# Attention over windows, products with V: one matmul for both heads of a pair, half of the result left unused, and two engines that copy the halves out

## The chip, the cores and the metric

One core of a Trainium2 chip runs the whole program. The metric is the time of one execution on the device, in microseconds (us); lower is better. TensorE (PE) multiplies, VectorE (DVE) and ScalarE (ACT) do elementwise work and copy results out of PSUM, GpSimd (POOL) does elementwise work in SBUF, and DMA queues move data.

## The reference, cut to what matters

A block with plain attention comes first, then six layers of local attention and a feed-forward network (FFN) over 4 x 1024 tokens of 128 features. The attention of a layer has 16 heads of 64 features and windows of 32 tokens, each of which looks at its own window and the one before it (64 keys):

```python
qkv = x @ Wqkv                                   # 128 -> 3 * 1024
# l2norm of q and k, rotary tables, then for each head and window of 32 queries:
sim = jnp.einsum('bhwie,bhwje->bhwij', bq, bk2) * QK_SCALE
sim = jnp.where(mask, -jnp.finfo(sim.dtype).max, sim)
attn = jax.nn.softmax(sim, -1)
out = jnp.einsum('bhwij,bhwje->bhwie', attn, bv2)
return out.reshape(b, h, n, d)                   # then @ Wo
```

The FFN is a layer norm, `x @ W1`, `a * gelu(gate)` and `@ W2`, each with a residual.

## The kernel before, in words

**Units and steps.** A unit is one tile of 128 tokens (four windows) with eight of the 16 heads (an `oct`), that is, four pairs of heads. There are 32 tiles x 2 octs x 6 layers = 384 units (`STEPS`). Everything is a software pipeline written out by hand: in each step, every engine does its part of several units, each at another stage, and semaphores (`need(engine, name, value)`) tie the engines together. There is no scheduler; each engine executes its list in the order in which it is written.

**TensorE in a step.** The loop at L893 to L907 issues, in this order: the first half of the FFN (`ffn_up`, L871 and L876) in one step of eight; the Q projection (L747, three matmuls of 512 columns); `ffn_down` (L886) in one step of eight; the scores (L767); the transpose of q (L779); the transpose of the probabilities (L800); the V projection and the K projection (L747); the transpose of k (L787); `attend(step-5)` (L824), the product with V; `output(step-6)` (L840), the product with Wo, in every second step; and the means of the FFN (L850, L857), each in one step of eight. There are 48 blocks of the FFN.

**attend.** For a pair `a` of heads, a window parity `w2`, a head `r` and a window half `wh`, one matmul holds V of one head as the stationary operand (64 keys by 64 features, rows `wh*64`) and streams the 32 queries of that head. The result goes to the partitions `r*64` of bank `6 + wh`. All operands are float32, for which the hardware executes each matmul of the source as two loads of the stationary operand and two matmuls; the 32 matmuls of the source are 64 loads and 64 matmuls in the trace. Each uses a quarter of the array, 64 rows by 64 columns, and four successive ones use the four quarters.

**attended.** ScalarE copies the 128 x 512 result of unit `n` to `aoT` (L471) one step later, and counts `aot_ready`. TensorE waits for that count ahead of the next `attend`, of `output`, and of `ffn_up`, whose results go into the banks 6 and 7 as well.

**VectorE in a step.** In order: the reciprocal of a sum (L1109), the K half of the rotation (L1085 to L1087), parts of the FFN in one step of eight each, the residual (L1095, in every second step, waits for `output`), the sum of the probabilities (L1103), `guarded` (L1070), `ffn_gated` (L1138, one step of eight), the row maximum (L1115, waits for the scores), the subtraction (L1123), the Q half of the rotation and two sums of squares (L1061).

Of the kernel before, what the change touches and what calls it, by code (L numbers as in the profile page):

```python
# [18 lines left out]
ACT = mybir.ActivationFunctionType  # L19
AX = mybir.AxisListType  # L20

P = 128
# [45 lines left out]
def is_unit(n):  # L68
    return 0 <= n < STEPS


def build(nc, x, w_attn, b_qk, b_v, Wqkv, Wo, W1, W2, cols, b1_cols, gains, c_t, wmod, rot_tab, out):
    ctx = ExitStack()
    with ctx:
# [3 lines left out]
        def sem(name):  # L78
# [94 lines left out]
            wqkv_in wo_in w1_in w2_in  # L173
            sqq_ready sqk_ready ssq_ready ssk_ready sg_ready ln_ready rn_ready rotq_ready rotk_ready add_ready qkr_ready trq_ready trk_ready seed_ready bits_set
            q_ready qk_ready sim_ready max_ready sub_ready p_ready pt_ready pts_ready vp_ready vs_ready pv_ready
            ri_ready aot_ready wo_ready x_mid_ready rot_made wo_moved pn_ready xs_ready w_hi w_lo sum_ready
            f_x f_m f_xc f_sq f_v f_ln f_rs f_xn f_xnT f_gate f_a f_gel f_u f_y f_out
            y_ready y_tr yo_ready y_sent""".split()
        s = {n: sem(n) for n in names}
# [7 lines left out]
        def need(eng, what, value):  # L187
            if value > 0:
                eng.wait_ge(s[what], value)
# [188 lines left out]
        def _(act):  # L378
# [86 lines left out]
            def attended(n):  # L465
                if not is_unit(n):
                    return
                tp, oc = n // UPT % 2, n % UPT
                need(act, "pv_ready", n + 1)
                need(act, "wo_ready", n // UPT - 1)  # L470
                act.activation(aoT[:, tp, oc * PAIRS:(oc + 1) * PAIRS, :].rearrange("p a (h n) -> p a h n", h=2),  # L471
                               psum[:, 6:8, 0:256].rearrange("p h (a n) -> p a h n", n=64), ACT.Copy).then_inc(s["aot_ready"], 1)

            def inverse_norm(n):
                if not is_unit(n):
# [167 lines left out]
        def _(pe):  # L643
# [167 lines left out]
            def attend(n, ffn_in_67):  # L811
                if not is_unit(n):
                    return
                tp, oc = n // UPT % 2, n % UPT
                pe.wait_ge(vsh_in[n % 4], (n // 4 + 1) * 32)
                need(pe, "pts_ready", n + 1)
                need(pe, "aot_ready", n)
                if ffn_in_67 is not None:
                    pe.wait_ge(s["f_u"], ffn_in_67 * CH + CH)
                for a in range(PAIRS):  # L820
                    for w2 in range(2):
                        for r in range(2):
                            for wh in range(2):
                                mm = pe.matmul(bank[6 + wh][r * 64:r * 64 + 64, a * 64 + w2 * WIN:a * 64 + w2 * WIN + WIN],  # L824
                                               vwin[w2][wh * 64:wh * 64 + 64, tp, oc, (2 * a + r) * DH:(2 * a + r + 1) * DH],
                                               probT[wh * 64:wh * 64 + 64, a, w2 * 64 + r * WIN:w2 * 64 + r * WIN + WIN],
                                               start=True, stop=True)
                mm.then_inc(s["pv_ready"], 1)

            def output(n):  # L830
                if not is_unit(n) or n % UPT == 0:
                    return
                tp, tile = n // UPT % 2, n // UPT
                need(pe, "aot_ready", n + 1)
                need(pe, "vs_ready", min(n + 4, STEPS))
                need(pe, "x_mid_ready", tile)
                if tile % TILES == 0:
                    pe.wait_ge(s["wo_moved"] if tile else s["wo_in"], tile // TILES if tile else 16)
                for k in range(HEADS // 2):
                    mm = pe.matmul(bank[5][:, 0:P], wo[:, k, :], aoT[:, tp, k, :],  # L840
                                   start=(k == 0), stop=(k == HEADS // 2 - 1))
                mm.then_inc(s["wo_ready"], 1)
# [16 lines left out]
            def ffn_up(b):  # L859
                if b is None:  # L860
                    return
                step = (b + 2) * UNROLL + 4
                layer = b // BLOCKS
                pe.wait_ge(s["w1_in"], layer * 16 + 16)
                pe.wait_ge(s["f_xnT"], b + 1)
                need(pe, "f_u", b * CH)
                need(pe, "pts_ready", min(step - 5, STEPS))
                need(pe, "aot_ready", min(step - 5, STEPS))
                for ch in range(CH):
                    w = CW[ch]  # L870
                    pe.matmul(bank[FFN_BANKS[ch]][0:w, :], w1[:, DFF + ch * P:DFF + ch * P + w], ff_n[:, :],  # L871
                              start=True, stop=True).then_inc(s["f_gate"], 1)
                for ch in range(CH):
                    w = CW[ch]
                    pe.wait_ge(s["f_gel"], b * CH + ch + 1)
                    pe.matmul(bank[FFN_BANKS[ch]][0:w, :], w1[:, ch * P:ch * P + w], ff_n[:, :],  # L876
                              start=True, stop=True).then_inc(s["f_a"], 1)
# [43 lines left out]
        def _(dve):  # L921
# [142 lines left out]
            def guarded(n):  # L1064
                if not is_unit(n):
                    return
                need(dve, "ssq_ready", n + 1)
                need(dve, "ssk_ready", n + 1)
                need(dve, "ln_ready", n)
                dve.tensor_reduce(ssg[:, :], ssq[:, :, :], AX.X, ALU.max).then_inc(s["sg_ready"], 1)  # L1070
# [18 lines left out]
            def residual(n):  # L1089
                if not is_unit(n) or n % UPT == 0:  # L1090
# [4 lines left out]
                dve.tensor_tensor(x_mid[:, col + 1:col + 1 + P], bank[5][:, 0:P], xs_in[:, col + HIST:col + HIST + P],  # L1095
                                  ALU.add).then_inc(s["x_mid_ready"], 1)

            def probability_sum(n):
                if not is_unit(n):
                    return  # L1100
                need(dve, "p_ready", n + 1)
                need(dve, "pn_ready", n - 1)
                dve.tensor_reduce(psumr[:, n % 2, 0, :], prob[:, n % 2, :, :], AX.X, ALU.add).then_inc(s["sum_ready"], 1)  # L1103
# [28 lines left out]
            def ffn_gated(b):  # L1132
                if b is None:
                    return
                for ch in range(CH):
                    w = CW[ch]
                    dve.wait_ge(s["f_a"], b * CH + ch + 1)
                    dve.scalar_tensor_tensor(out=gel[0:w, ch, :], in0=bank[FFN_BANKS[ch]][0:w, :],  # L1138
                                             scalar=b1_col[0:w, b // BLOCKS, 0, ch:ch + 1], in1=gel[0:w, ch, :],
                                             op0=ALU.add, op1=ALU.mult).then_inc(s["f_u"], 1)  # L1140
# [11 lines left out]
            for step in range(STEPS + 2 * UNROLL):  # L1152
                inverse_sum(step - 5)
                rotation(step - 1, 1)
                ffn_centred(block_at(step, 1))
                ffn_out(block_at(step, 5))
                residual(step - 7)
                probability_sum(step - 4)
                guarded(step - 1)
                ffn_gated(block_at(step, 4))  # L1160
                row_maximum(step - 3)
                below_maximum(step - 3)
                rotation(step, 0)
                square_sum(step, 0)
                square_sum(step, 1)
# [76 lines left out]
```

## Time and profile before

| | |
|---|---|
| median of three runs | 3431.78 us (3429.99 to 3432.28) |
| the profiled execution | 3432.49 us, span 3430.7 us |
| granted TensorE clock, mean | 0.987 |
| PE matmul / PE weight load busy | 96% / 75% of the span |
| DVE / ACT / POOL busy | 77% / 78% / 69% |
| matmuls and loads of the product with V (L824) | 24576 of each |

The span is the time from the first to the last instruction; the time of the run is 1.8 us more. "PE" are matmuls and "PEld" the loads of the stationary operand, which can go on beside a matmul. A busy PE isn't yet a PE at its peak, since the recorded time of a matmul includes the way through the array: a matmul that is recorded with 219 ns can be followed by another on the same quarter after much less than that. The rates must be read from starts, not from durations.

### The profile page before, as it was taken

What the parts mean: (1) busy time and instruction counts of PE and PEld (TensorE: products, weight loads), DVE (VectorE), ACT (ScalarE), POOL (GpSimd) and SP (SyncE); (2) the same over time, 40 slices, a digit from 0 to 9 for tenths busy, and PEclk for the clock granted to TensorE, in tenths of its full rate; (3) what the DMA queues carried; (4) which work ended last, traced back from release to release, by engine and by line L of the source; (5) the groups of instructions that cost most, each with busy time, mean ns of one, the idle gap of its engine ahead of it and who ended that gap; (6) DMA issues with size and microseconds to landing.
All of it is one profiled execution on the core that took longest, in us unless ns stands there. A gap on an engine that the chain in (4) does not pass through costs nothing. (4 is left out here: it accounts for less than half of the span.)

```text
span 3430.7 us, 124638 instructions
## 1 busy us (share of the span) xinstructions
PE 3290.3 (96%) x50165; PEld 2578.9 (75%) x50165; DVE 2628.7 (77%) x5823; ACT 2683.1 (78%) x5501; POOL 2361.1 (69%) x1568
## 2 busy tenths in 40 slices
PE   7979999999999999999999999999999999999997
PEld 5758777777777777777777777777777777777774
DVE  4558878878878877887877887877788777788783
ACT  3438888888888887888888888888888888888884
POOL 2028767777777776776777777777677677777771
PEclk9989999999999999999999999999999999999998
DMA  2001111211111211111211211121111121111111
GB/s 85 2 6 50 44 37 46 68 39 50 42 41 45 69 41 39 53 44 36 71 42 38 53 43 40 43 67 44 44 46 43 39 71 39 47 44 45 41 40 46
DMA packets 98187, 156.44 MB, mean 46 GB/s; under 512 B 18128, under 2 KB 39632, under 8 KB 96720
## 3 DMA queue, kind: packets, MB, share of 16 engines
q1 hardware_dynamic: 93440, 132.73, 14.3%
q10 hardware_dynamic: 4176, 15.74, 1.4%
q8 instruction: 402, 6.59, 0.8%
q14 instruction: 169, 1.38, 0.1%
HBM read 20.48 MB, written 2.10 MB: 7 GB/s over the span
## 5 line engine op out<-in xcount | busy, mean ns | idle before, releaser
L314 POOL TENSOR_TENSOR qks<-work 128x1024 f32<-128x1024 f32 x384 | 910.0, 2370 | 72.0 <-issue 62.8
L322 POOL TENSOR_TENSOR qkr<-qks,rnorm 128x1024 f32<-128x1024 f32 x384 | 731.4, 1905 | 321.0 <-issue 296.9
L330 POOL TENSOR_TENSOR probn<-prob,psumr 128x512 f32<-128x512 f32 x384 | 400.6, 1043 | 390.5 <-DVE psumr L1109 390.5
L498 ACT ACTIVATE sq<-psum 128x512 f32<-128x512 f32 x768 | 464.9, 605 | 184.1 <-PE psum L747 180.6
L747 PE MATMUL psum<-whi,xhi 128*128 128x512 f32 x1152 | 563.5, 489 | 20.5 <-POOL xlo L339 14.6
L1085 DVE TENSOR_TENSOR work<-psum,rot 128x512 f32<-128x512 f32 x768 | 508.1, 662 | 63.9 <-POOL qks L314 52.1
L1061 DVE TENSOR_REDUCE ssq<-sq 128x8 f32<-128x512 f32 x768 | 514.1, 679 | 42.6 <-ACT sq L498 16.0
L767 PEld LDWEIGHTS psum<-kT,qbd 128*64 128x64 f32 x12288 | 393.6, 139 | 172.2 <-issue 136.7
L747 PE MATMUL psum<-whi,xlo 128*128 128x512 f32 x1152 | 459.7, 399 | 0.0
L767 PE MATMUL psum<-kT,qbd 128*64 128x64 f32 x12288 | 447.0, 226 | 12.4 <-ACT kT L534 12.4
L747 PE MATMUL psum<-wlo,xhi 128*128 128x512 f32 x1152 | 455.9, 396 | 0.0
L1115 DVE TENSOR_REDUCE nmax<-psum 128x8 f32<-128x512 f32 x384 | 264.5, 689 | 201.2 <-PE psum L767 199.1
L840 PE MATMUL psum<-aoT,wo 128*128 128x128 f32 x3072 | 395.3, 282 | 0.0
L824 PE MATMUL psum<-probT,vsh 64*64 64x32 f32 x12288 | 391.3, 222 | 1.9 <-ACT probT L515 1.7
L824 PE MATMUL psum<-probT,vtok 64*64 64x32 f32 x12288 | 383.7, 219 | 0.0
L824 PEld LDWEIGHTS psum<-probT,vsh 64*64 64x64 f32 x12288 | 327.2, 134 | 67.3 <-issue 67.3
L840 PEld LDWEIGHTS psum<-aoT,wo 128*128 128x128 f32 x3072 | 358.9, 192 | 8.3 <-issue 0.5
L507 ACT ACTIVATE qbd<-psum 64x512 f32<-64x512 f32 x384 | 224.9, 586 | 145.7 <-PE psum L779 140.3
L824 PEld LDWEIGHTS psum<-probT,vtok 64*64 64x64 f32 x12288 | 329.3, 135 | 0.0
L1086 DVE TENSOR_TENSOR work<-psum,rot 128x256 f32<-128x256 f32 x768 | 317.8, 414 | 0.0
L1087 DVE TENSOR_TENSOR work<-psum,rot 128x256 f32<-128x256 f32 x768 | 317.3, 413 | 0.0
L747 PEld LDWEIGHTS psum<-whi,xhi 128*128 128x128 f32 x1152 | 219.0, 190 | 82.0 <-issue 34.7
(132 smaller groups left out, 6496.2 us busy)
## 6 DMA issues: line engine op xcount, KB each, us to landing
vsh<-vtok SPq DMA_DIRECT2D x384, 192.0 KB, 2.4
vsh<-vtok SPq DMA_DIRECT2D x384, 64.0 KB, 2.9
xsh<-xs_in SPq DMA_DIRECT2D x192, 64.0 KB, 2.4
ff_x<-x_mid SPq DMA_DIRECT2D x96, 128.0 KB, 2.4
wqkv<-Wqkv_dram ACTq DMA_DIRECT2D x5, 1536.0 KB, 7.6
wo_next<-Wo_dram ACTq DMA_DIRECT2D x5, 512.0 KB, 9.6
xtok<-x_dram SPq DMA_DIRECT2D x4, 512.0 KB, 10.9
out_dram<-qkr SPq DMA_DIRECT2D x8, 256.0 KB, 2.6
```

What stands on the lines that cost most here:

```text
L314: pool.tensor_tensor(qks[:, :, :], rcos, rsin, ALU.add).then_inc(s["add_ready"], 1)
L322: pool.tensor_tensor(qkr[:, n % 2, :, :], qks[:, :, :], rnorm[:, :].unsqueeze(2).to_broadcast([P, 2 * OCT, DH]), ALU.mult).then_inc(s["qkr ...
L330: pool.tensor_tensor(probn[:, :, :], prob[:, n % 2, :, :], psumr[:, n % 2, 1, :].unsqueeze(2).to_broadcast([P, OCT, KEYS]), ALU.mult).then ...
L498: act.activation(sq[:, w * OCT:(w + 1) * OCT, :], bank[w].rearrange("p (h n) -> p h n", n=DH), ACT.Square).then_inc(s[("sqq_ready", "sqk_r ...
L747: mm = pe.matmul(out, xparts[xp][:, ti, :], wparts[wp_][:, w, oc * 512:(oc + 1) * 512], start=(k == 0), stop=(k == 2))
L767: mm = pe.matmul(bank[3][w % 2 * 64:w % 2 * 64 + 64, c:c + KEYS], qbd[:, a, w, :, :].rearrange("p r n -> p (r n)"), kT[:, oc * PAIRS + a, ...
L824: mm = pe.matmul(bank[6 + wh][r * 64:r * 64 + 64, a * 64 + w2 * WIN:a * 64 + w2 * WIN + WIN], vwin[w2][wh * 64:wh * 64 + 64, tp, oc, (2 * ...
L840: mm = pe.matmul(bank[5][:, 0:P], wo[:, k, :], aoT[:, tp, k, :], start=(k == 0), stop=(k == HEADS // 2 - 1))
L1061: dve.tensor_reduce(ssq[:, w * OCT:(w + 1) * OCT, 0], sq[:, w * OCT:(w + 1) * OCT, :], AX.X, ALU.add).then_inc(s[("ssq_ready", "ssk_ready" ...
L1085: dve.tensor_tensor(rc, x3, table(0, 0, DH), ALU.mult)
L1086: dve.tensor_tensor(rs[:, :, 0:H], x3[:, :, H:DH], table(1, 0, H), ALU.mult)
L1087: dve.tensor_tensor(rs[:, :, H:DH], x3[:, :, 0:H], table(1, H, H), ALU.mult).then_inc(s[("rotq_ready", "rotk_ready")[w]], 1)
```

## The change

The product with V takes both heads of a pair at once. The stationary operand is V of both heads (64 keys by 128 features), and the moving operand is the 64 columns of both heads' probabilities. The result has 128 partitions (features of both heads) by 64 columns (queries of both heads), of which the two blocks on the diagonal are wanted and the two others aren't. It is written so that the columns of head 0 go to the first half of the bank and those of head 1 to the second half. The matmuls of the source fall from 32 to 16 for a unit. ScalarE then copies the partitions 0 to 63 of the first half (64 x 512), and VectorE, in the new `attended_upper`, the partitions 64 to 127 of the second half (64 x 512), and counts `aod_ready`. TensorE waits for this count too, at the three places at which it waits for `aot_ready`.

```diff
@@ attended (ScalarE)
-                act.activation(aoT[:, tp, oc * PAIRS:(oc + 1) * PAIRS, :].rearrange("p a (h n) -> p a h n", h=2),
-                               psum[:, 6:8, 0:256].rearrange("p h (a n) -> p a h n", n=64), ACT.Copy).then_inc(s["aot_ready"], 1)
+                act.activation(aoT[0:64, tp, oc * PAIRS:(oc + 1) * PAIRS, :].rearrange("p a (h n) -> p a h n", h=2),
+                               psum[0:64, 6:8, 0:256].rearrange("p h (a n) -> p a h n", n=64), ACT.Copy).then_inc(s["aot_ready"], 1)
@@ attend (TensorE)
                 need(pe, "aot_ready", n)
+                need(pe, "aod_ready", n)
...
                 for a in range(PAIRS):
                     for w2 in range(2):
-                        for r in range(2):
-                            for wh in range(2):
-                                mm = pe.matmul(bank[6 + wh][r * 64:r * 64 + 64, a * 64 + w2 * WIN:a * 64 + w2 * WIN + WIN],
-                                               vwin[w2][wh * 64:wh * 64 + 64, tp, oc, (2 * a + r) * DH:(2 * a + r + 1) * DH],
-                                               probT[wh * 64:wh * 64 + 64, a, w2 * 64 + r * WIN:w2 * 64 + r * WIN + WIN],
-                                               start=True, stop=True)
+                        for wh in range(2):
+                            c = a * 64 + w2 * WIN
+                            mm = pe.matmul(bank[6 + wh].rearrange("p (r c) -> p r c", r=2)[:, :, c:c + WIN],
+                                           vwin[w2][wh * 64:wh * 64 + 64, tp, oc, 2 * a * DH:2 * (a + 1) * DH],
+                                           probT[wh * 64:wh * 64 + 64, a, w2 * 64:w2 * 64 + 64],
+                                           start=True, stop=True)
                 mm.then_inc(s["pv_ready"], 1)
@@ output (TensorE)
                 need(pe, "aot_ready", n + 1)
+                need(pe, "aod_ready", n + 1)
@@ ffn_up (TensorE)
                 need(pe, "aot_ready", min(step - 5, STEPS))
+                need(pe, "aod_ready", min(step - 5, STEPS))
@@ VectorE
+            def attended_upper(n):
+                if not is_unit(n):
+                    return
+                tp, oc = n // UPT % 2, n % UPT
+                need(dve, "pv_ready", n + 1)
+                need(dve, "wo_ready", n // UPT - 1)
+                dve.tensor_copy(aoT[64:P, tp, oc * PAIRS:(oc + 1) * PAIRS, :].rearrange("p a (h n) -> p a h n", h=2),
+                                psum[64:P, 6:8, 256:512].rearrange("p h (a n) -> p a h n", n=64)).then_inc(s["aod_ready"], 1)
...
                 guarded(step - 1)
+                attended_upper(step - 6)
                 ffn_gated(block_at(step, 4))
```

On TensorE the whole of `attend` for one unit stands between the transpose of k (L787) and the product with Wo or a mean of the FFN. Before, as the program lists it (the sizes are those of the output, `vsh` and `vtok` hold V of the shifted and the plain tile):

```order
L824 MATMUL psum<-probT,vsh 64x32 [waits aot_ready,pts_ready,vsh_in3]
L824 MATMUL psum<-probT,vsh 64x32 x3
L824 MATMUL psum<-probT,vtok 64x32 x4
L824 MATMUL psum<-probT,vsh 64x32 x4
L824 MATMUL psum<-probT,vtok 64x32 x4
L824 MATMUL psum<-probT,vsh 64x32 x4
L824 MATMUL psum<-probT,vtok 64x32 x4
L824 MATMUL psum<-probT,vsh 64x32 x4
L824 MATMUL psum<-probT,vtok 64x32 x4
L850 MATMUL psum<-ff_x,mean_mat 128x512 [waits pts_ready,f_out,f_x]
```

Of the changed kernel, the same stretch with a product with Wo (now L842) behind it:

```order
L825 MATMUL psum<-probT,vsh 128x2x32 [waits aot_ready,aod_ready,pts_ready,vsh_in2]
L825 MATMUL psum<-probT,vsh 128x2x32
L825 MATMUL psum<-probT,vtok 128x2x32 x2
L825 MATMUL psum<-probT,vsh 128x2x32 x2
L825 MATMUL psum<-probT,vtok 128x2x32 x2
L825 MATMUL psum<-probT,vsh 128x2x32 x2
L825 MATMUL psum<-probT,vtok 128x2x32 x2
L825 MATMUL psum<-probT,vsh 128x2x32 x2
L825 MATMUL psum<-probT,vtok 128x2x32 x2
L842 MATMUL psum<-aoT,wo 128x128 [waits vs_ready,x_mid_ready,aod_ready,aot_ready]
```

Where four matmuls of 64 x 32 stood there are now two of 128 x 64, and the first waits for one semaphore more.

On VectorE, in the step of an FFN block in which TensorE does `ffn_up`, the program before lists from the residual on:

```order
L1095 TENSOR_TENSOR x_mid<-psum,xs_in 128x128 [waits wo_ready]
L1103 TENSOR_REDUCE psumr<-prob 128x8 [waits pn_ready,p_ready]
L1070 TENSOR_REDUCE ssg<-ssq 128x16 [waits ln_ready,ssk_ready,ssq_ready]
L1138 SCALAR_TENSOR_TENSOR gel<-psum,b_col,gel 128x512 [waits f_a] x2
L1138 SCALAR_TENSOR_TENSOR gel<-psum,b_col,gel 85x512 [waits f_a]
```

The changed program, whose line numbers are 3 to 12 higher there, lists:

```order
L1098 TENSOR_TENSOR x_mid<-psum,xs_in 128x128 [waits wo_ready]
L1115 TENSOR_REDUCE psumr<-prob 128x8 [waits pn_ready,p_ready]
L1073 TENSOR_REDUCE ssg<-ssq 128x16 [waits ln_ready,ssk_ready,ssq_ready]
L1107 COPY aoT<-psum 64x512 [waits wo_ready,pv_ready]
L1150 SCALAR_TENSOR_TENSOR gel<-psum,b_col,gel 128x512 [waits f_a] x2
L1150 SCALAR_TENSOR_TENSOR gel<-psum,b_col,gel 85x512 [waits f_a]
```

The copy stands fourth, behind three instructions the first of which waits for the product with Wo, and ahead of the gating of the FFN. TensorE's list in that step shows who waits for it:

```order
L842 MATMUL psum<-aoT,wo 128x128 x7
L874 MATMUL psum<-ff_n,w 128x512 [waits pts_ready,aot_ready,f_u,aod_ready,f_xnT,w1_in]
```

The first matmul of `ffn_up` (L871 before, L874 now) stands directly behind the product with Wo and now names `aod_ready`, the count of that copy.

## Rows read from the trace of the kernel before

**Rows 1.** The page, busy time by engine, and the granted TensorE clock in 40 slices

```profile
PE 3290.3 (96%) x50165; PEld 2578.9 (75%) x50165; DVE 2628.7 (77%) x5823; ACT 2683.1 (78%) x5501; POOL 2361.1 (69%) x1568
...
PEclk9989999999999999999999999999999999999998
```

**Rows 2.** Waits: engine, line, releaser: us in total, times, longest

```profile
DVE nmax L1115 <- PE psum L767: 199.1, 234, 3.6
...
PE psum L871 <- ACT aoT L471: 40.5, 46, 0.9
```

**Rows 3.** Timeline, weight loads around one product with V: start us, us, what

```profile
1706.48 0.21 PEld L824 LDWEIGHTS psum<-probT,vsh 64*64 64x64 f32 x8 [0.17 <-issue]
...
1707.29 0.21 PEld L824 LDWEIGHTS psum<-probT,vtok 64*64 64x64 f32 x8
1707.55 1.86 PEld L840 LDWEIGHTS psum<-aoT,wo 128*128 128x128 f32 x16
1709.33 0.19 PEld L747 LDWEIGHTS psum<-whi,xhi 128*128 128x128 f32 x1
```

**Rows 4.** Timeline, matmuls of the same stretch

```profile
1707.32 0.30 PE L824 MATMUL psum<-probT,vtok 64*64 64x32 f32 x8
...
1707.55 2.05 PE L840 MATMUL psum<-aoT,wo 128*128 128x128 f32 x16
...
1709.36 0.48 PE L747 MATMUL psum<-whi,xhi 128*128 128x512 f32 x1
```

**Rows 5.** Timeline, one block of scores and the start of what follows

```profile
1702.55 1.15 PE L767 MATMUL psum<-kT,qbd 128*64 128x64 f32 x32
...
1703.63 0.65 PE L779 MATMUL psum<-ident,qkr 128*128 128x128 f32 x4
```

**Rows 6.** Timeline, loads and matmuls of a projection behind a product with V

```profile
1701.65 0.19 PEld L747 LDWEIGHTS psum<-whi,xhi 128*128 128x128 f32 x1
1701.65 0.50 PE L747 MATMUL psum<-whi,xhi 128*128 128x512 f32 x1
1701.76 0.19 PEld L747 LDWEIGHTS psum<-wlo,xhi 128*128 128x128 f32 x1
...
1701.98 0.40 PE L747 MATMUL psum<-wlo,xhi 128*128 128x512 f32 x1
```

**Rows 7.** Groups of weight loads by shape: busy us, mean ns, idle before

```profile
L767 PEld LDWEIGHTS psum<-kT,qbd 128*64 128x64 f32 x12288 | 393.6, 139 | 172.2 <-issue 136.7 <-ACT kT L534 35.3
L840 PEld LDWEIGHTS psum<-aoT,wo 128*128 128x128 f32 x3072 | 358.9, 192 | 8.3 <-issue 0.5
...
L824 PEld LDWEIGHTS psum<-probT,vsh 64*64 64x64 f32 x12288 | 327.2, 134 | 67.3 <-issue 67.3
```

**Rows 8.** Timeline of a step with `ffn_up`

```profile
1738.50 0.29 DVE L1095 TENSOR_TENSOR x_mid<-psum,xs_in 128x128 f32<-128x128 f32 x1 [0.26 <-PE psum L840]
1738.59 0.61 ACT L471 ACTIVATE aoT<-psum 128x512 f32<-128x512 f32 x1
1738.70 0.68 DVE L1103 TENSOR_REDUCE psumr<-prob 128x8 f32<-128x512 f32 x1
...
1739.30 0.18 DVE L1070 TENSOR_REDUCE ssg<-ssq 128x16 f32<-128x32 f32 x1
...
1739.34 2.81 PE L871 MATMUL psum<-ff_n,w 128*128 128x512 f32 x6 [0.88 <-ACT aoT L471]
```

**Rows 9.** Groups by shape on DVE: a plain copy out of PSUM

```profile
L1008 DVE COPY qkr<-psum 128x512 f32<-128x512 f32 x32 | 21.8, 682 | 0.9 <-PE psum L701 0.8
```

**Rows 10.** Groups by shape on ACT: copies of 128 and of 64 partitions

```profile
L515 ACT ACTIVATE probT<-psum 128x512 f32<-128x512 f32 x384 | 229.8, 598 | 12.1 <-PE psum L800 2.7
...
L507 ACT ACTIVATE qbd<-psum 64x512 f32<-64x512 f32 x384 | 224.9, 586 | 145.7 <-PE psum L779 140.3
```

**Rows 11.** Windows of two steps: us, busy us (count) by engine, clock, DMA

```profile
1701.65:1709.35 7.70, 7.70 (x139) 6.70 (x134) 7.02 (x17) 7.36 (x17) 6.59 (x5) 1.00 0.64 167
1715.24:1721.98 6.74, 6.74 (x124) 5.27 (x119) 6.53 (x15) 5.96 (x15) 5.96 (x4) 1.00 0.15 43
```

More of the change, by code:

```diff
@@ L175, in build @@
             q_ready qk_ready sim_ready max_ready sub_ready p_ready pt_ready pts_ready vp_ready vs_ready pv_ready
-            ri_ready aot_ready wo_ready x_mid_ready rot_made wo_moved pn_ready xs_ready w_hi w_lo sum_ready
+            ri_ready aot_ready aod_ready wo_ready x_mid_ready rot_made wo_moved pn_ready xs_ready w_hi w_lo sum_ready
             f_x f_m f_xc f_sq f_v f_ln f_rs f_xn f_xnT f_gate f_a f_gel f_u f_y f_out
```

## The prediction

> **What bounds the kernel now.** I read the page first. TensorE is busy 96% of the span, no other engine over 78%, and the clock is at the upper of its two levels (2.4 GHz) in nearly all slices [rows 1]. The list of waits says the same from the other side: the largest wait of TensorE's matmuls is 40.5 us in 46 pieces, for ScalarE's copy of `aoT` ahead of `ffn_up`, while VectorE waits 199 us for the scores alone [rows 2]. So the kernel lasts as long as TensorE's list, and any time that `attend` takes is paid 384 times. VectorE's idle time costs nothing unless TensorE waits for VectorE.
>
> What an `attend` costs must be read from starts, since loads and matmuls overlap. The first load starts at 1706.48, the product with Wo behind it at 1707.55: 1.07 us for a block [rows 3], 384 of them 411 us, 12% of the span.
>
> **What sets these 1.07 us.** A block is 64 loads and 64 matmuls, sixteen of each on every quarter of the array. The first eight loads start at 1706.48, the eighth group of eight at 1707.29: 0.81 us for seven groups, 0.116 us for a group, which is two loads per quarter. So a quarter takes a new load every 0.058 us, and all four work side by side [rows 3]. Is that the load, or the matmul? The scores tell the matmul's part: there each matmul streams 64 columns instead of 32 on one of two halves, and the block of 32 takes 1.08 us to the next block [rows 5], again sixteen per half, the same 0.058 us. Twice the streamed columns at the same pace: in `attend` the streaming of 32 columns can't be what limits. Loads of 64 columns are common to both.
>
> The product with Wo has loads of 128 columns and matmuls of 128 columns, sixteen in sequence on the whole array. From its first load to the next block's load is 1.78 us [rows 3], 0.111 us each. That alone doesn't say whether load or matmul limits. A projection behind a product with V does: its first matmul is recorded with 0.50 us where the next has 0.40, and the second load starts 0.11 us after the first [rows 6], at a moment when nothing else is in the array. The first matmul stands there waiting for its stationary operand, and a load of 128 columns occupies its place for 0.10 to 0.11 us at full clock. The recorded durations agree: 134 and 139 ns for 64 columns, 192 ns for 128 columns, 53 to 58 ns more for 64 more columns. And rows don't matter: 64 rows (L824) and 128 rows (L767) with 64 columns are 5 ns apart [rows 7].
>
> **The change on TensorE.** It halves the matmuls of the source, but doubles the columns of each load, and leaves half as many places in the array: two halves of 64 rows by 128 columns instead of four quarters. Each half gets 8 matmuls of the source, so sixteen loads and sixteen matmuls, as each quarter had. What changes is the pace, from 0.058 us (64 columns) to 0.111 us (128 columns), while its matmuls stream 64 columns, which the scores show to fit into 0.058 us. The two halves run side by side, as the rows of quarters do now. So the block's length is that of sixteen successive loads of 128 columns, 1.78 us, by the row of L840, and then the way from the last matmul's start to the next block. For L824 that is 0.15: the last group of matmuls starts at 1707.32 and lasts 0.30, of which the last is 0.22, so it starts at 1707.40, and the next block at 1707.55 [rows 4]. Together 1.93; with one half's first instruction behind the other's, and 64 columns instead of 32 in the last matmul, 1.94 us. More by 0.87 us, times 384: **+334 us**.
>
> The Trainium skill, TensorE: Matmul & The Clock Gate, section LDWEIGHTS, has this as a rule: the time of a load is its columns over 1.2 GHz, whatever the number of rows, and it speaks against the change: 53 ns would become 107 ns. The trace agrees (0.058 and 0.111 us of pace). By its figures alone the sum would be 16 x 53 ns x 384, an estimate of +328 us.
>
> **The change on ScalarE and VectorE.** ScalarE's copy shrinks from 128 to 64 partitions and keeps its 512 elements for each. A copy of 128 x 512 is 598 ns, one of 64 x 512 586 ns [rows 10]: nothing is saved. VectorE gets 384 copies of 64 x 512 out of PSUM. The nearest row is a copy of 128 x 512 out of PSUM, 682 ns [rows 9]; as partitions hardly matter, 0.68 us of record, some 0.6 us of VectorE's time as successive instructions overlap by about 0.08 (1738.70 + 0.68 against 1739.30 in [rows 8]). In the steps without an FFN that is hidden: VectorE is busy 7.02 of 7.70 us in a step with a product with Wo and 6.53 of 6.74 in one with a mean of the FFN [rows 11], and the copy stands ahead of the wait for the scores, which is where VectorE idles (199 us, [rows 2]). TensorE's own added 0.87 us per step is more than VectorE's 0.6 us, so VectorE gains slack in every step. Without this cover (TensorE not slower), the 0.6 us would exceed VectorE's idle time in some steps; the upper bound is 384 x 0.6 = 230 us less the 199 us, some 30 us.
>
> **The one new wait.** `ffn_up` needs the banks 6 and 7 and so both copies. Today it starts when ScalarE's copy ends: 1738.59 + 0.61 = 1739.20, TensorE at 1739.34, 0.14 later [rows 8]. Behind the change VectorE comes last. Its copy stands behind the residual, which waits for the product with Wo, then the sum and `guarded`. In [rows 8] `guarded` starts at 1739.30 for 0.18 us; the copy would start at 1739.40, end at 1740.08, and TensorE start at 1740.22, **0.88 us later**. Since that chain begins with TensorE's own product with Wo, it moves along with TensorE: slack that ScalarE gains from a slower `attend` doesn't help. There are 48 blocks, the last without this overlap: 47 x 0.88 = **+41 us**. Queued behind the waiting matmul is the whole step, so all of it counts. The added wait in `attend` and `output` costs nothing: the copy ends 1.6 us behind the residual's start (1738.50 to 1740.08), which follows the product with Wo, and from there to the next `attend` TensorE has 7.70 - 1.07 - 1.78 = 4.85 us of other work in a step of 7.70 us [rows 11]; in the steps without a residual the copy is earlier.
>
> **Sum.** Against the profiled execution, 3432.5 us (0.7 over the median): 3432.5 + 334 + 41 = 3807.5, rounded **3808 us**, 1.11 times the time before.
>
> **The rivals.**
>
> *The load isn't what limits, the stream is.* If a load over 64 rows and 128 columns costs no more than one of 64 columns, the pace is that of the scores: 1.08 us for a block against 1.07. Then 384 x 0.01 = 4, plus the wait's 41, plus up to 30 for a VectorE that isn't covered: 3478 to 3508 us, likeliest **3480**. For it: transposes load 128 columns faster than others do, so 128 columns aren't bound to a fixed time. Against it: [rows 6] and [rows 7], where every ordinary load of 128 columns takes the longer time. Chance 0.08.
>
> *The number of instructions is what limits* (the faster side). In a block 64 loads and 64 matmuls take 1.07 - 0.15 = 0.92 us, 7.2 ns for an instruction. If the issue set that, 64 instructions would take 0.46: 384 x 0.46 = 177 us less, plus 41: **3297 us**. It decides for "faster" as soon as a block falls under 1.07 - 41/384 = 0.96 us. Against it, the scores: 64 instructions take 1.08 - 0.15 = 0.93 us there, not 0.46 [rows 5]. Chance 0.03. The Trainium skill, TensorEngine Tiling, section Instruction Overhead, points this way too: a matmul of few columns costs about as much as one of 60, so that one of 64 in place of two of 32 would be nearly free of charge. The trace doesn't bear it out as the limit here, since quarters take a matmul of 32 and halves one of 64 at the same pace.
>
> *The two halves don't load side by side.* If loads over all columns exclude each other, 32 of them take 32 x 0.111 = 3.55 us, a block 3.70: 384 x 2.63 = 1010 more, plus 41: **4484 us**. Against it: today's quarters of the same columns but other rows do overlap (a load every 0.0145 us, each 0.05 long). Chance 0.04.
>
> *Something between*, as a switch of the array's shape that gets cheaper or dearer: the entry into the scores costs, by [rows 5] and [rows 3], no more than 0.15 at either end; a block's ends can move by 0.1 us each way, 38 us in all. It is in the range of my forecast.
>
> **How the numbers follow.** My forecast has a chance of 0.85. Its own range: 0.1 us for each block (38 us) and the wait between nothing and 47 x 1.1 = 52 us, so from 3808 - 38 - 41 = 3729, and as both low together is unlikely, 3745, up to 3808 + 38 + 11 = 3857, rounded 3855. That holds 0.81. The rivals lie far off on both sides and are left out, so this is also the range for 8 in 10. Slower by over 0.2% (about 7 us, what a measurement of this kernel tells from no change): the forecast, the stream rival, and the serial one, 0.965. Faster: 0.03. Same: 0.005.
>
> **What would show it.** In the profile after: the loads of the product with V at about 190 ns instead of 134; a block at 1.94 us from its first load to the next block's (1.08 if the stream limits, 0.6 if the issue does, 3.7 if the halves exclude each other); VectorE's copies at 0.6 to 0.69 us; in the list of waits, `ffn_up` waiting for VectorE's copy and not ScalarE's, some 1.7 us each time instead of 0.88, about 80 us in all; VectorE's wait for the scores no smaller than 199 us less 230 plus the slack that TensorE gives; TensorE's clock unchanged. The prediction is wrong if the block isn't within 0.1 us of 1.94, or if a wait shows up on TensorE that isn't named here, at ScalarE above all, whose 7.36 busy us of 7.70 [rows 11] are the fullest.

## The result, and the profile after

The changed kernel takes **3839.66 us** in the median of four runs (3836.29 to 3842.36), against 3431.63 us before (four runs, 3429.99 to 3432.28): 1.1192 times as long, 95% interval 1.1178 to 1.1206. That lies within the range that was predicted (3745 to 3855), 32 us above the predicted 3808.

The page shows TensorE as the bound again: 95% busy, with 366 us more of matmuls in 406 us more of span, and a quarter fewer instructions ([rows 1] for before):

```profile
PE 3656.1 (95%) x37877; PEld 2909.0 (76%) x37877; DVE 2902.9 (76%) x6207; ACT 2685.1 (70%) x5501; POOL 2359.7 (62%) x1568
...
PEclk9989999999999999999999999999999999999998
```

The timeline of the weight loads around one product with V, now L825, answers to [rows 3]:

```profile
1779.12 0.30 PEld L825 LDWEIGHTS psum<-probT,vsh 64*128 64x128 f32 x4 [0.17 <-issue]
...
1780.68 0.31 PEld L825 LDWEIGHTS psum<-probT,vtok 64*128 64x128 f32 x4
1781.06 1.75 PEld L842 LDWEIGHTS psum<-aoT,wo 128*128 128x128 f32 x15
```

A block lasts 1781.06 - 1779.12 = 1.94 us instead of 1.07; seven groups of four loads, two per half, take 1.56 us, so a half takes a new load every 0.111 us. From matmul to matmul the block is 1.932 us in the median of all 384, and 1.065 before. The group of the loads answers to [rows 7], VectorE's new copy to [rows 9]:

```profile
L825 PEld LDWEIGHTS psum<-probT,vsh 64*128 64x128 f32 x6144 | 470.1, 188 | 66.9 <-issue 66.9
```

```profile
L1107 DVE COPY aoT<-psum 64x512 f32<-64x512 f32 x384 | 266.6, 694 | 12.0
```

In the list of waits, the wait of `ffn_up` (L874 now) answers to the second of [rows 2]. ScalarE's 40.5 us are gone, VectorE's copy has taken their place:

```profile
DVE nmax L1127 <- PE psum L767: 92.5, 99, 1.9
PE psum L874 <- DVE aoT L1107: 88.2, 47, 2.1
```

One such place in the timeline, to be read against [rows 8]:

```profile
1782.36 0.58 ACT L471 ACTIVATE aoT<-psum 64x512 f32<-64x512 f32 x1
...
1783.15 0.29 DVE L1098 TENSOR_TENSOR x_mid<-psum,xs_in 128x128 f32<-128x128 f32 x1 [1.14 <-PE psum L842]
...
1783.36 0.67 DVE L1115 TENSOR_REDUCE psumr<-prob 128x8 f32<-128x512 f32 x1
1783.95 0.17 DVE L1073 TENSOR_REDUCE ssg<-ssq 128x16 f32<-128x32 f32 x1
1784.15 0.69 DVE L1107 COPY aoT<-psum 64x512 f32<-64x512 f32 x1
...
1784.99 4.51 PE L874 MATMUL psum<-ff_n,w 128*128 128x512 f32 x6 [1.89 <-DVE aoT L1107]
```

ScalarE is done at 1782.94, beside the end of the product with Wo. VectorE waits for that product, then does the residual, the sum and `guarded`, and ends the copy at 1784.84. From the start of the last matmul with Wo to the start of the first of `ffn_up` it is 2.16 us (47 places, median), 1.16 before; the last matmul itself is 0.28 of it, so that TensorE idles for 1.88 us, and for 0.88 before. The wait at `ffn_up` is given from start to start from here on.

The last row shows something that the prediction doesn't have: six matmuls take 4.51 us, where [rows 8] has 2.81. Three windows of the same place, with busy times by engine and the granted clock (behind POOL), tell why:

```profile
1782.90:1784.90 2.00, 0.21 (x2) 0.02 (x1) 1.67 (x4) 1.32 (x2) 2.00 (x2) 1.00 0.01 4
1785.75:1789.10 3.35, 3.35 (x5) 1.21 (x4) 0.00 (x0) 1.37 (x2) 0.00 (x0) 0.50 0.00 0
1789.20:1792.00 2.80, 2.80 (x8) 1.15 (x7) 1.49 (x2) 1.97 (x2) 0.00 (x0) 1.00 0.03 6
```

TensorE works for 0.21 of 2.00 us while it waits, and 0.75 us after `ffn_up` has begun its clock falls from 2.4 to 1.2 GHz for 3.4 us, right in the matmuls with 512 columns. The trace's record of the clock has such a stretch behind 24 of the 47 waits. In the kernel before none of the 47 waits at `ffn_up`, 0.88 us idle each, has one behind it. It has four elsewhere, each behind the other long wait of TensorE, at the start of a layer, where there are five of 1.93 to 1.95 us; here is one, and the clock behind it:

```profile
1777.72 0.50 PE L747 MATMUL psum<-whi,xhi 128*128 128x512 f32 x1 [1.94 <-POOL xlo L339]
...
1778.60:1781.90 3.30, 3.30 (x40) 3.17 (x40) 1.22 (x2) 1.14 (x4) 3.22 (x3) 0.50 0.00 0
```

In the changed kernel these five waits are 1.07 us, as TensorE's steps are longer, and have no such stretch behind them. From the first matmul of `ffn_up` to the next `attend` it takes 11.65 us with such a stretch and 9.95 us without.

The 406 us by which the span grew, from the starts of TensorE's matmuls in both traces:

| part | us |
|---|---|
| 384 blocks of `attend`, 0.867 us each | +332 |
| wait between the product with Wo and `ffn_up`, 1.0 us more in 47 places | +48 |
| matmuls of `ffn_up`, at the lower clock in 24 places | +41 |
| all else | -15 |

The last row is mostly the starts of the layers: in the step before and in the first step TensorE's waits are some 0.87 us shorter each, in five places (9 us), and the four stretches at the lower clock are gone, 1.5 us each (6 us).

### The profile page after: what moved, and what is told of

It reads as the page before. It is cut to its first block and busy times, and to the rows that moved or that the text cites. A ratio compares the mean times of both kernels' runs of the same rounds, so it can differ in the third digit from the quotient of the medians.

```text
span 3836.8 us, 101396 instructions
## 1 busy us (share of the span) xinstructions
PE 3656.1 (95%) x37877; PEld 2909.0 (76%) x37877; DVE 2902.9 (76%) x6207; ACT 2685.1 (70%) x5501; POOL 2359.7 (62%) x1568
## 5 line engine op out<-in xcount | busy, mean ns | idle before, releaser
L825 PE MATMUL psum<-probT,vsh 64*128 64x64 f32 x6144 | 618.9, 278 | 1.8 <-ACT probT L515 1.7
L825 PE MATMUL psum<-probT,vtok 64*128 64x64 f32 x6144 | 600.5, 272 | 0.0
L825 PEld LDWEIGHTS psum<-probT,vsh 64*128 64x128 f32 x6144 | 470.1, 188 | 66.9 <-issue 66.9
L825 PEld LDWEIGHTS psum<-probT,vtok 64*128 64x128 f32 x6144 | 472.1, 189 | 0.0
L842 PE MATMUL psum<-aoT,wo 128*128 128x128 f32 x3072 | 393.9, 282 | 1.6 <-issue 1.6
L842 PEld LDWEIGHTS psum<-aoT,wo 128*128 128x128 f32 x3072 | 357.4, 192 | 15.3 <-issue 2.4
L1150 DVE SCALAR_TENSOR_TENSOR gel<-psum,b_col,gel 128x512 f32<-128x512 f32 x144 | 107.9, 749 | 244.5 <-PE psum L879 234.2
```

The lines of the kernel that those rows point to most:

```text
L825: mm = pe.matmul(bank[6 + wh].rearrange("p (r c) -> p r c", r=2)[:, :, c:c + WIN], vwin[w2][wh * 64:wh * 64 + 64, tp, oc, 2 * a * DH:2 * ( ...
```

## The experiments

Two theories stood against each other at first. **A**: 333 us from the pace of the loads, 47 us from the new wait, and the rest from a clock that falls because of that wait. **B**: the rest comes from VectorE's added work, or from something spread over all steps. Each comparison below is with the kernel before on the same chip.

**Experiment 1, VectorE's copy before the residual.**

```diff
                 rotation(step - 1, 1)
+                attended_upper(step - 6)
...
                 guarded(step - 1)
-                attended_upper(step - 6)
```

> The changed kernel, with VectorE's copy moved ahead of the residual (so no longer behind the product with Wo). Theory A: of the 408 us, 333 are the longer products with V, 47 the wait of ffn_up for this copy (1.00 us more in 47 places), and the rest (some 26 to 39 us) a TensorE clock that falls to its lower level behind the 2.16 us of that wait, in 24 of the 47 places. Then without the wait the time falls by all that ffn_up now waits (1.9 us in 47 places, 90 us, since ScalarE's copy has slack beside a slower TensorE) and by the clock's 39 us: 3711 us, 3700 to 3730, and no stretch at the lower clock in the middle of the layers. Rival B: the rest comes from VectorE's added load or from TensorE's work all over the steps: then only the wait goes, 3750 us, and the clock goes on falling.

Measured: 3713.51 us, ratio 1.0821 (1.0805 to 1.0837). The timeline of VectorE shows the copy 1.1 us ahead of the residual instead of behind it:

```profile
1731.11 0.70 DVE L1107 COPY aoT<-psum 64x512 f32<-64x512 f32 x1
1732.21 0.29 DVE L1098 TENSOR_TENSOR x_mid<-psum,xs_in 128x128 f32<-128x128 f32 x1 [0.40 <-PE psum L842]
```

and that of TensorE the product with Wo and `ffn_up` nearly without a gap, its six matmuls in 2.81 us again:

```profile
1730.12 2.05 PE L842 MATMUL psum<-aoT,wo 128*128 128x128 f32 x16
1732.27 2.81 PE L874 MATMUL psum<-ff_n,w 128*128 128x512 f32 x6
```

The wait fell from 2.16 to 0.37 us, and no stretch at the lower clock is left behind it. The place of one VectorE instruction in the list is worth 126 us: 47 x 1.79 = 84 us of wait and 41 of clock. The copy itself costs as much time on VectorE as in the changed kernel (695 ns), so B is out.

**Experiment 2, the copies without the matmuls.** `attend` has the 32 matmuls of before, and VectorE copies from the first half of the bank:

```diff
-                                psum[64:P, 6:8, 256:512].rearrange(...)
+                                psum[64:P, 6:8, 0:256].rearrange(...)
```

> The matmuls of before (quarters of the array, 64 columns loaded, 32 streamed), with the copies of the change alone: ScalarE copies the partitions 0 to 63, VectorE 64 to 127, at the place of the change. Theory A: a block stays at 1.065 us; ffn_up waits 1.00 us more in 47 places (47 us), and as the wait is as long as in the changed kernel, the clock falls in some of them, 0 to 40 us: 3479 to 3520 us. Rival B: VectorE isn't covered by a slower TensorE and becomes a bound in the steps without an FFN: up to 30 us more, and waits of TensorE for the rotations (L747 on work) show up in the list.

Measured: 3518.97 us, ratio 1.0260 (1.0243 to 1.0277): 87 us for the split alone, at the upper end. The waits:

```profile
PE psum L874 <- DVE aoT L1107: 88.2, 47, 2.1
DVE nmax L1127 <- PE psum L767: 59.8, 53, 2.8
...
PE psum L747 <- DVE work L1090: 7.1, 5, 2.8
```

The wait at `ffn_up` is that of the changed kernel to 0.1 us. The stretches at the lower clock are 24 again, but 21 of them are behind this wait and 3 at the starts of layers, behind waits of 1.94 us as in the kernel before. 48 us of wait and 21 x 1.7 = 36 us of clock are 84 of the 87 us. VectorE's idle time ahead of the row maximum shrinks from 199 us [rows 2] to 60 us: it takes up 139 of the some 230 us that the prediction gave the copies. TensorE's wait for the rotations is 7.1 us against 5.9 before, so VectorE doesn't become a bound even without a slower `attend`.

**Experiment 3, the matmuls without the split.** `attend` as changed, with the kernel's single ScalarE copy (L471) and no copy on VectorE. The upper half of `aoT` then gets values of the unused part.

> The matmuls of the change (halves of the array, 128 columns loaded, 64 streamed) with the single ScalarE copy of before. It copies 128 partitions of the columns of head 0 alone, so the upper half of aoT holds values of the unused part of the result: the output isn't that of the reference, the work is the same. Theory A: +333 us for the blocks (1.932 us), no wait for VectorE, and the wait of ffn_up for ScalarE nearly gone since TensorE's steps are longer (1.13 us in 47 places before, 53 us less): 3432 + 333 - 50 = 3715 us, 3700 to 3735. Rival: ScalarE's copy stays the last in those steps, 3765 us.

Measured: 3708.29 us, ratio 1.0809 (1.0793 to 1.0825). The timeline of TensorE has the product with Wo and `ffn_up` 0.03 us apart:

```profile
1726.70 2.05 PE L840 MATMUL psum<-aoT,wo 128*128 128x128 f32 x16
1728.78 2.81 PE L871 MATMUL psum<-ff_n,w 128*128 128x512 f32 x6
```

332 us of longer blocks are paid, but 55 us come back. 40 of them are the wait of `ffn_up` for ScalarE, 1.16 us before and now 0.30, since ScalarE keeps its pace beside a slower TensorE; the rest is what the changed kernel has at the starts of its layers too. Matmuls alone cost 277 us, copies alone 87, both 408: of the 44 us that are missing, 40 are the gain that the late VectorE copy hides, and 3 more stretches at the lower clock than in experiment 2 are most of the others.

**Experiment 5, 128 columns loaded, 32 streamed.** Only the columns of head 0 are streamed; head 1's part is left out.

```diff
-                                           probT[wh * 64:wh * 64 + 64, a, w2 * 64:w2 * 64 + 64],
+                                           probT[wh * 64:wh * 64 + 64, a, w2 * 64:w2 * 64 + WIN],
```

> The changed kernel with 128 columns loaded but only the 32 columns of head 0 streamed (VectorE copies from the first half of the bank as well). Head 1's part of the output is left out, so the output isn't that of the reference. Theory A (the load sets the pace): a block keeps its 16 x 0.111 us, 1.90 to 1.93 us, and the kernel 3825 to 3840 us. Rival (the stream of 64 columns sets or shares the pace): the block falls towards 1.0 us and the kernel by up to 350 us.

Measured: 3821.21 us, ratio 1.1137 (1.1121 to 1.1154), 4 us under the expected range. The loads of one block:

```profile
1801.23 0.30 PEld L825 LDWEIGHTS psum<-probT,vsh 64*128 64x128 f32 x4 [0.17 <-issue]
...
1802.79 0.31 PEld L825 LDWEIGHTS psum<-probT,vtok 64*128 64x128 f32 x4
1803.13 0.19 PEld L747 LDWEIGHTS psum<-whi,xhi 128*128 128x128 f32 x1
```

The pace is the same 1.56 us for seven groups, and the block 1.905 us, 27 ns shorter. Half of the streamed columns is worth 10 us, a further 8 to 10 us go with 18 stretches at the lower clock instead of 24. The stream doesn't set the pace, the load does. The width of the result goes with the columns of the load, 128 partitions instead of 64, but writing it isn't the limit: six matmuls of `ffn_up` write 512 columns of 128 partitions each in 2.81 us [rows 8], 0.47 us for one, where experiment 5 writes 32 in 0.111.

**Experiment 4, quarters with 64 columns streamed.** The reverse, to be compared with experiment 2 (3519 us): 64 columns loaded in quarters, but both heads' columns streamed.

```diff
-                                mm = pe.matmul(bank[6 + wh][r * 64:r * 64 + 64, a * 64 + w2 * WIN:a * 64 + w2 * WIN + WIN],
+                                mm = pe.matmul(bank[6 + wh][r * 64:r * 64 + 64, :].rearrange("p (q c) -> p q c", q=2)[:, :, a * 64 + w2 * WIN:a * 64 + w2 * WIN + WIN],
...
-                                               probT[wh * 64:wh * 64 + 64, a, w2 * 64 + r * WIN:w2 * 64 + r * WIN + WIN],
+                                               probT[wh * 64:wh * 64 + 64, a, w2 * 64:w2 * 64 + 64],
```

> The split copies of the change, with quarters of the array again: 32 matmuls of the source, 64 columns loaded, but 64 streamed (both heads' probabilities, half of the result unused). Against the run with before's matmuls and split copies (3519 us) only the streamed columns double. Theory A (pace of a quarter is the larger of the load, 53 ns, and the stream, 53 ns, plus some 5): a block lasts 1.08 to 1.10 us instead of 1.065, so 5 to 15 us more: 3524 to 3534 us. Rival (all streams of the array share one path): the block lengthens towards 1.9 us and the kernel by 300 us.

Measured: 3533.70 us, ratio 1.0300 (1.0285 to 1.0315). In the loads of one block, seven groups of eight take 0.81 us, as in [rows 3]:

```profile
1802.81 0.21 PEld L825 LDWEIGHTS psum<-probT,vsh 64*64 64x64 f32 x8 [0.17 <-issue]
...
1803.62 0.21 PEld L825 LDWEIGHTS psum<-probT,vtok 64*64 64x64 f32 x8
1803.91 1.86 PEld L842 LDWEIGHTS psum<-aoT,wo 128*128 128x128 f32 x16
```

Twice the stream costs 27 ns for a block (1.092 us), 10 us in all; the other 5 us against experiment 2 fit its 24 instead of 21 stretches at the lower clock behind `ffn_up`. So of the two things that the change doubles for a place in the array, the streamed columns are nearly free and the loaded ones cost all of the 333 us.

**Experiment 6, the halves in turn.** The changed kernel with the loop over `wh` outside:

```diff
-                for a in range(PAIRS):
-                    for w2 in range(2):
-                        for wh in range(2):
+                for wh in range(2):
+                    for a in range(PAIRS):
+                        for w2 in range(2):
```

> The changed kernel with the loop over the two halves of the rows (wh) outside: eight matmuls of the source on one half of the array, then eight on the other. Nothing else changes. Theory A (a half takes a new load of 128 columns every 0.111 us, and the changed kernel has two halves going side by side): 32 loads in succession, a block of 3.6 to 3.8 us, 384 x 1.75 = 670 us more: 4480 to 4560 us. Rival: TensorE reaches ahead to the other half and the block stays near 1.93 us, 3840 us.

Measured: 4576.95 us, ratio 1.3346 (1.3316 to 1.3375). The loads of one block, in the timeline:

```profile
1799.39 0.29 PEld L825 LDWEIGHTS psum<-probT,vsh 64*128 64x128 f32 x2 [0.17 <-issue]
...
1800.51 0.30 PEld L825 LDWEIGHTS psum<-probT,vtok 64*128 64x128 f32 x2
1800.73 0.35 PEld L825 LDWEIGHTS psum<-probT,vsh 64*128 64x128 f32 x4
1800.95 0.35 PEld L825 LDWEIGHTS psum<-probT,vtok 64*128 64x128 f32 x4
...
1802.35 0.30 PEld L825 LDWEIGHTS psum<-probT,vtok 64*128 64x128 f32 x2
1802.71 1.42 PEld L842 LDWEIGHTS psum<-aoT,wo 128*128 128x128 f32 x12
```

Two loads in 0.22 us where the changed kernel does four: the halves did go side by side, and only if neighbouring instructions belong to different halves. Where the list passes from one half to the other, at 1800.73, eight loads fall into 0.5 us, so TensorE does reach ahead to the other half, but over a few instructions only. That fits a block of 3.32 us instead of the 3.6 to 3.8 that were expected. The total lies 17 us above the expected range all the same: the blocks account for 384 x 1.387 = 533 us of the 737 us more than the changed kernel, and the clock was at the lower level in 142 stretches between the first and the last product with V, instead of 24 (mean 0.933 against 0.980). They are the rest. Between the blocks, set against the same steps of the changed kernel, the 121 steps with another share of the lower clock take 195 us more, and the 262 with the same share 5 us less.

**Experiment 8, work in the wait.** The changed kernel, with the Q projection ahead of `ffn_up`:

```diff
-                ffn_up(block_at(step, 4))
                 projection(step, 0)
+                ffn_up(block_at(step, 4))
```

> The changed kernel with TensorE's Q projection ahead of ffn_up instead of behind it, in the steps with ffn_up. The copy is as late as in the change, but TensorE works during a part of the wait. Theory A: 0.79 us of the 2.16 are filled, 47 x 0.79 = 37 us less, and if it is the idle stretch that makes the clock fall, the 24 stretches at the lower level vanish too, 39 us less: 3764 us (3755 to 3775). Rival: the clock falls for what ffn_up itself does, then the stretches stay: 3803 us.

Measured: 3767.06 us, ratio 1.0982 (1.0963 to 1.1000), 73 us less than the change. The wait that is left:

```profile
PE psum L874 <- DVE aoT L1107: 56.4, 47, 1.4
```

It fell from 88.2 to 56.4 us, that is by 32 us, or from 1.88 to 1.20 us in one place, and no stretch at the lower clock is left behind it, which is the other 41 us. `ffn_up` is the same, and so is VectorE's list: what the clock falls for is the length of the idle stretch ahead, not what `ffn_up` does itself.

**Experiments 7, 9, 10 and 11, from the kernel before.** The wait of 1.16 us at `ffn_up` is in the kernel before too. In the step with `ffn_up`, 7 puts ScalarE's copy and `ffn_affine` first; 11 puts `k_turned` behind the gelus in addition; 9 puts the projection first, as in experiment 8; 10 is 7 and 9 together.

```diff
+                first = block_at(step, 4) is not None
+                if first:
+                    attended(step - 6)
+                    ffn_affine(block_at(step, 4))
                 k_turned(step - 3)
                 exponential(step - 4)
-                ffn_affine(block_at(step, 4))
                 ffn_inverse(block_at(step, 3))
-                attended(step - 6)
+                if not first:
+                    attended(step - 6)
```

> The kernel before with another order on ScalarE in the step of ffn_up alone: the copy of aoT and ffn_affine stand ahead of k_turned and exponential. Theory A (today ffn_up waits 1.16 us from the last matmul with Wo, for ScalarE): both are done by about the end of the product with Wo, the wait falls to 0.3 to 0.5 us, 47 x 0.75 = 35 us less, between 3385 and 3405 us. Rival: what ScalarE does later there is waited for in turn (kT by the scores, prob by VectorE), and the time stays at 3430.

> The kernel before with TensorE's Q projection ahead of ffn_up in the steps with ffn_up. ffn_up waits 1.16 us there for ScalarE's copy; the projection fills 0.79 of it: 47 x 0.79 = 37 us less, 3394 us (3388 to 3405). Rival: the gelu and the gating behind it come 0.8 us later and TensorE waits for them in turn, 3430 us.

> Both edits together: ScalarE's copy and ffn_affine first, and TensorE's Q projection ahead of ffn_up. With the first alone the wait at ffn_up fell from 1.16 to 0.11 us (49 us in all), but the time by 33 us, since TensorE then waits 0.3 us longer for the first gelu. With the projection ahead that wait is filled as well: 3432 - 49 = 3383 us (3378 to 3392). Rival: no better than either alone, 3395 us.

> ScalarE's order as in the earlier run (3399 us), with k_turned behind the three gelus in the steps with ffn_up, and TensorE's order as before. The table load and the first gelu come 0.5 us earlier, so TensorE's 0.3 us of wait for it goes: 3399 - 47 x 0.3 = 3385 us. Rival: the scores wait for kT in turn, since k_turned then ends at about the end of the Q projection: 3400 us or more.

Measured: 7, 3399.03 us, ratio 0.9908 (0.9893 to 0.9923); 9, 3395.17, 0.9898 (0.9884 to 0.9911); 11, 3379.86, 0.9854 (0.9841 to 0.9868); 10, **3374.09**, 0.9837 (0.9824 to 0.9851), the fastest here and 466 us under the change. In experiment 7 the timeline of TensorE shows the wait ahead of `ffn_up` (L875 there) gone and a small one behind it, until the first gelu (L880 starts 2.96 us after L875; in the kernel before the same distance is 2.65):

```profile
1723.43 2.81 PE L875 MATMUL psum<-ff_n,w 128*128 128x512 f32 x6
1726.39 2.41 PE L880 MATMUL psum<-ff_n,w 128*128 128x512 f32 x5
```

In experiment 10 there is neither:

```profile
1712.55 0.40 PE L751 MATMUL psum<-whi,xlo 128*128 128x512 f32 x1
1712.79 2.74 PE L875 MATMUL psum<-ff_n,w 128*128 128x512 f32 x6
1715.36 2.74 PE L880 MATMUL psum<-ff_n,w 128*128 128x512 f32 x6
```

Experiments 7 and 9 came out as expected: 32 and 36 us less. Both 10 and 11 came out faster than expected, by 9 and 5 us, 10 below its range. The stretches at the lower clock at the starts of layers fell from 4 to 1 in experiment 10, which at 1.5 us each is some 4 of its 9 us; the rest wasn't traced further.

## Why the prediction was right, and where its sum was short

The cost that carries the sum came out, and with it the time. That the median also lies within the range is in part luck: the room above the sum, 38 and 11 us, was meant for longer blocks and a longer wait, which took 5 us together; a clock term of 41 us that nobody had thought of filled most of it, and the starts of the layers gave 15 us back, equally unforeseen.

**The loads set the pace of `attend`: right.** The step that carried the sum, sixteen successive loads of 128 columns in place of sixteen of 64, gave 1.94 us and 334 us; measured were 1.932 and 332. The argument had three parts, and each is borne out: the stream isn't the limit (experiments 4 and 5), two halves load side by side (6), and rows don't matter to a load of 128 columns (188 ns for 64 rows, 192 ns for 128, by the records of the changed kernel). One reading behind it was weaker than it was put. In [rows 6] the array was not empty: the last matmuls with V are recorded until 1701.72, 0.07 us into that load.

```profile
1701.42 0.30 PE L824 MATMUL psum<-probT,vtok 64*64 64x32 f32 x8
```

The experiments, not this row, show that the load limits. The Trainium skill states that a load takes its columns over 1.2 GHz (TensorE: Matmul & The Clock Gate, LDWEIGHTS). The trace agrees: the pace went from 0.058 to 0.111 us where that rule gives 0.053 and 0.107, and the estimate of 328 us from its figures is 4 us under the measured 332.

**The number of instructions: right to leave out.** Half as many instructions gave no time back: 32 matmuls take 1.93 us where 64 took 1.07. The Trainium skill (TensorEngine Tiling, Instruction Overhead) states that a matmul of one column takes as long as one of 60. Experiment 4 doesn't speak against that, since 64 columns in place of 32 add only 27 ns to a block; but it isn't the limit here, or the changed kernel's block would have become shorter.

**ScalarE gains nothing: right**, 614 to 587 ns for half of the partitions. VectorE's copy is 694 ns, against 682 predicted.

**The new wait: right in place and mechanism, sized low.** The term was 47 x 0.88 = 41 us; the list of waits has 88.2 - 40.5 = 48. `guarded` and the copy start 0.20 us apart where 0.10 was assumed.

**The clock: missing.** The prediction said that TensorE's clock would be unchanged. It counted a wait at its own length only. At 1.88 us of idle TensorE the clock fell behind half of the waits, and 24 x 1.7 = 41 us were added that no term had. This is the step that failed. With 7 us more for the wait, 2 less for the blocks and the 15 that the starts of the layers gave back, it makes 31 us, which is the distance of the profiled run (3838.55) from 3807.5. Experiments 1 and 8 show it: with the wait gone, or partly filled with work, the stretches go. Why 24 of the waits have one and 23 don't, at the same length, no run shows.

**VectorE without cover: the upper bound of 30 us was too careful.** Experiment 2 has the cover taken away, and the copy still costs TensorE nothing but the wait at `ffn_up` and the clock behind it.

## What to carry to other kernels

Where TensorE does many small matmuls, count for each place in the array its successive loads times their columns: joining two matmuls into one of twice the stationary columns halves the instructions and nearly doubles the time, as here from 1.07 to 1.93 us, while streaming twice the columns added 27 ns to a block. And when a result is handed to a second engine, look at what stands ahead of the new copy in that engine's list at the one point where a slower engine waits for it: here the place of a copy was worth 126 us, the copy itself 5 (experiment 1 against 3). Where the wait can't go, put independent work of TensorE ahead of it.

## What the runs showed of the hardware that had not been expected

- Idle stretches of TensorE of 1.88 us, one in each 73 us, made the clock fall to 1.2 GHz for 3.4 us in 24 of 47 places (21 and 24 in experiments 2 and 4, 18 in experiment 5), and those of 1.94 us at the starts of layers in 4 of 5 places of the kernel before. Behind the 47 of 0.88 us in the kernel before, the 47 of 1.20 us in experiment 8 and the 5 of 1.68 us ahead of the scores in either kernel it never fell.
- The clock falls without any wait too. In experiment 6 TensorE is 96% busy, but one half of the array works at a time in `attend`, and the mean granted clock is 0.933, with 142 stretches at the lower level. In 126 of them TensorE had no idle stretch of over 0.3 us in the 7 us ahead; 94 begin in the product with Wo, which stands right behind `attend`, and 27 in `attend` itself.
- TensorE overlaps loads of different halves across a few neighbouring instructions only (experiment 6: eight loads in the 0.5 us at the joint, two in each 0.22 us elsewhere). The order in which a kernel lists its halves is worth 737 us here, of which some 195 are the clock.
